# A vision tower on one core: four buffers for a head's exponentials, column copies in pairs, tile list and last side steps moved

## The reference, cut to what matters

```python
for i in range(L):                                   # L = 4 layers, H = 16 heads of 64
    q, k, val = split(h @ W_qkv[i])
    kr = r @ W_r[i]                                  # position keys
    AC = einsum("bqhd,bkhd->bhqk", q + u, k)
    BD = einsum("bqhd,khd->bhqk", q + v, kr)
    prob = softmax((AC + BD) * inv_sqrt_d)           # 257 x 257 for each image and head
    vec = einsum("bhqk,bkhd->bqhd", prob, val)
    h = layer_norm(h + vec @ W_o[i])
    h = layer_norm(relu(h @ W_ff1[i] + b1) @ W_ff2[i] + b2)
...
w = macro_top1 * micro_top2                          # each row: one group of four, its two experts
out = einsum("te,tef,efd->td", w, silu(x @ gate_w[e]) * (x @ up_w[e]), down_w)
```

## Time and profile before

| What | Value |
|---|---|
| Time, median of 3 runs | 2613.9 us (2610.91 to 2614.98) |
| The profiled execution: time, span | 2615.31 us, 2613.5 us |
| PE busy | 2233.3 us, 85% of the span |
| DVE busy | 1846.4 us, 71% |
| ACT busy | 1614.7 us, 62% |
| POOL busy | 1187.9 us, 45% |
| The chain that ended last, by engine | PE 34%, ACT 31%, DVE 11%, issue 7%, POOL 5%, SP's queue 4% |
| Its costliest line | ACT L2144 (exponentials), 12% |
| Mean granted TensorE clock | 0.973 |

### The profile page before, as it was taken

The page is one execution under the profiler, slowest core; times in us unless marked ns, Lnnn a source line. Parts: engine busy times, 40 slices in busy tenths (PEclk is TensorE's granted clock), DMA queues, the critical chain, the costliest instruction groups (busy, mean ns, idle before and its releaser), DMA issues.

```text
span 2613.5 us, 61377 instructions
## 1 busy us (share of the span) xinstructions
PE 2233.3 (85%) x19254; PEld 1641.1 (63%) x19254; DVE 1846.4 (71%) x5687; ACT 1614.7 (62%) x5077; POOL 1187.9 (45%) x2205
## 2 busy tenths in 40 slices
PE   0259999999989999999989999999899999987998
PEld 0136666666766666667656666667666666665565
DVE  8837777777767777777757777777678777776533
ACT  2126667767666677776656667766676766665322
POOL 3025555555456555554544555554565555541211
PEclk9679999999999999999999999999999999998999
DMA  4344444435554343444644444445543343355110
GB/s 162 88 136 112 113 103 105 105 99 145 143 157 119 99 102 102 103 122 132 183 117 115 105 104 104 104 139 143 157 100 91 86 102 90 94 144 178 50 45 22
DMA packets 378062, 295.38 MB, mean 113 GB/s; under 512 B 45087, under 2 KB 350721, under 8 KB 376739
## 3 DMA queue, kind: packets, MB, share of 16 engines
q1 hardware_dynamic: 370603, 272.41, 39.9%
q10 hardware_dynamic: 4864, 12.68, 1.4%
q0 software_dynamic: 2272, 6.35, 0.7%
HBM read 137.71 MB, written 72.07 MB: 80 GB/s over the span
## 4 chain that ended last, share of the span: by engine, by line
PE 34%; ACT 31%; DVE 11%; issue 7%; POOL 5%; SPq 4%; DMA 1%; ACTq 0%; POOLq 0%; DVEq 0%
ACT e_rows L2144 12%; PE bk L2024 6%; PE bk L1898 6%; PE bk L2059 4%; PE bk L1273 4%; ACT pt L2129 4%; SPq L1532 3%; ACT pt L2204 3%; ACT rel L2079 3%; ACT rel L2203 2%; DVE pt L2445 2%; PE bk L2048 2%; POOL arena L1726 2%; PE bk L1886 2%; PE bk L1854 2%
## 5 line engine op out<-in xcount | busy, mean ns | idle before, releaser
L2144 ACT ACTIVATE e_rows<-e_rows,nb 128x257 f32<-128x257 f32 x1024 | 518.0, 519 | 40.8 <-DVE nb L2334 39.9
L2334 DVE CUSTOM_DVE_ANT_0 e_rows<-bk,arena 128x257 f32<-128x257 f32 x1024 | 390.0, 418 | 72.6 <-PE bk L1931 71.4
L1838 PE MATMUL bk<-hin,arena 128*128 128x257 f16 x3072 | 424.0, 275 | 10.2 <-ACT rel L2079 6.6
L2296 DVE TENSOR_TENSOR pt<-bk,pt 128x512 f16<-128x512 f32 x512 | 353.8, 691 | 77.2 <-ACT pt L2129 70.1
L1886 PE MATMUL bk<-ident,e_rows 128*128 128x128 f32 x2048 | 325.0, 281 | 70.7 <-ACT e_rows L2144 52.4
L1724 POOL TENSOR_SCALAR arena<-rel 128x257 f16<-128x257 f32 x496 | 202.6, 409 | 356.2 <-ACT rel L2079 352.0
L1726 POOL TENSOR_TENSOR arena<-rel,arena 128x257 f16<-128x257 f32 x496 | 327.4, 660 | 41.3
L1838 PEld LDWEIGHTS bk<-hin,arena 128*128 128x128 f16 x3072 | 298.1, 98 | 61.2 <-issue 9.2
L1886 PEld LDWEIGHTS bk<-ident,e_rows 128*128 128x128 f32 x2048 | 221.2, 141 | 159.3 <-ACT e_rows L2144 131.4
L2129 ACT ACTIVATE pt<-bk 128x512 f16<-128x512 f32 x512 | 311.6, 609 | 8.1 <-PE bk L1886 8.0
L1774 POOL TENSOR_SCALAR wf<-wf 128x256 f32<-128x256 f32 x216 | 93.0, 431 | 424.6 <-DMA wf<-in_w_dram 254.1
(11 more groups left out here) (328 smaller groups left out, 4278.6 us busy)
## 6 DMA issues: line engine op xcount, KB each, us to landing
arena<-arena SPq DMA_DIRECT2D x768, 128.5 KB
wf<-in_w_dram SPq DMA_DIRECT2D x168, 128.0 KB, 2.9
w_split_dram<-wh SPq DMA_DIRECT2D x168, 128.0 KB, 2.2
xs_dram<-in_c_blank_dram SPq DMA_DIRECT2D x24, 772.5 KB
wf<-in_we_dram SPq DMA_DIRECT2D x96, 128.0 KB, 2.7
we_split_dram<-wh SPq DMA_DIRECT2D x96, 128.0 KB, 1.8
w_rest<-w_split_dram SPq DMA_DIRECT2D x12, 1024.0 KB, 17.0
arena<-we_split_dram SPq DMA_DIRECT2D x8, 1536.0 KB, 11.5
```

Source lines behind the costliest of these rows:

```text
L1838: r_ = mm(bank[4 + s % 2][:, 0:S], wcol(a, C_QKV, k, 3 * HD, chunk_at(s)), hin[:, m, k, :], start=i == 0, stop=i == 5)
L2144: act.activation(E[:, h % 2, qt, :], E[:, h % 2, qt, :], ACT.Exp, bias=nb[:, 2 * h + qt:2 * h + qt + 1], scale=-1.0, accum_out=sums[:, qt, ...
L2296: v.tensor_tensor(pt[:, h, 1, :, 0:IMG], bank[2 + h % 2][:, :].rearrange("p (k s) -> p k s", k=QT), pt[:, h, 0, :, 0:IMG], ALU.subtract).t ...
L2334: v.tensor_tensor_reduce(E[:, h % 2, qt, :], bank[qt][:, 0:S], cb[:, h, :], -SCORE, 3e38, ALU.add, ALU.min, nb[:, 2 * h + qt:2 * h + qt + ...
```

## The change

E gets four buffers (`h % EB`, EB = 4), and DVE waits for the transposes of head h-4 and for the copy of its pair. The column copy is made on odd heads alone, for both heads of a pair in one instruction. To make room, the small tables of the tile list move into the tile that held the position rows (`rT2`), which the last layer doesn't read; the loop that names them is cut below. `first_list` leaves heads 13 to 15 of FINAL and is spread over the value steps c = 0 to 6, two steps each. In the experts' loop several side steps change places.

```diff
+EB = 4
-        E = e_rows[:, 0:2 * QT * S].rearrange("p (b k s) -> p b k s", b=2, k=QT)
+        E = e_rows[:, :].rearrange("p (b k s) -> p b k s", b=EB, k=QT)
...
 # ACT, head h
-                    act.wait_ge(e_ok, at(32, 2 * h + 2))
-                    act.activation(ecol[:, :, class_row(h, 0):class_row(h, 3):4], E[:, h % 2, :, CLS:S].broadcast_to([P, QT, 3]), ACT.Copy).then_inc(ecol_ok, 1)
+                    if h % 2:
+                        act.wait_ge(e_ok, at(32, 2 * h + 2))
+                        both = E[:, (h - 1) % EB:(h - 1) % EB + 2, :, CLS].rearrange("p b k -> p k b").unsqueeze(2).broadcast_to([P, QT, 3, 2])
+                        first, i = class_row(h - h % 4, 0), (h - 1) % 4
+                        act.activation(ecol[:, :, first:first + 12].rearrange("p k (c i) -> p k c i", i=4)[:, :, :, i:i + 2], both, ACT.Copy).then_inc(ecol_ok, 1)
...
 # DVE, head h
-                    if h >= 2:
-                        v.wait_ge(t_done, at(16, h - 1))
-                        v.wait_ge(ecol_ok, at(16, h - 1))
+                    if h >= EB:
+                        v.wait_ge(t_done, at(16, h - EB + 1))
+                        v.wait_ge(ecol_ok, at(8, (h - EB) // 2 + 1))
...
-                    if kind is FINAL and h >= 13:
-                        for k in range(5 * (h - 13), min(5 * (h - 12), experts.LIST)):
-                            experts.first_list(v, k)
...
 # DVE, value step c
                     if c:
                         o_part(at, c - 1)
+                    if kind is FINAL and c < 7:
+                        for k in range(2 * c, min(2 * c + 2, experts.LIST)):
+                            experts.first_list(v, k)
...
 # Experts.vector, tile j
             if j == 3:
                 for k in range(NEWTON):
                     route_newton(v, r, LAST, k)
-                route_normalise(v, r, LAST)
...
             if j + 1 < SLOT_TILES:
                 inner(j + 1, 0)
-            if j == 0:
-                for k in range(WEIGHTS):
-                    route_weights(v, r, LAST - 1, k)
+            if j == 3:
+                route_normalise(v, r, LAST)
             if j == 5:
-                for k in range(WEIGHTS):
+                for k in range(4):
                     route_weights(v, r, LAST, k)
             inner_lo(j, 1)
+            if j + 2 < SLOT_TILES:
+                self.rows_lo(v, j + 2)
             if j == 0:
                 for k in range(SLOTS):
                     route_slots(v, r, LAST - 1, self.side, k)
             if j == 1:
                 add_image()
-            if j + 2 < SLOT_TILES:
-                self.rows_lo(v, j + 2)
             finish(j)
+            if j == 0:
+                for k in range(WEIGHTS):
+                    route_weights(v, r, LAST - 1, k)
...
             if j == 5:
+                for k in range(4, WEIGHTS):
+                    route_weights(v, r, LAST, k)
+            if j == 6:
                 self.next_list(v)
```

More of the change, by code:

```diff
@@ L941, in __init__, with small @@
         self.we = in_arena(keep["arena"], 0, [E_N, E_CHUNKS, 2 * SPLIT])
-        self.steps = sb("steps", [P, CAP + SLOT_TILES + 2 * E_G])
-        self.count = sb("slot_count", [P, E_G])
-        self.cmp = sb("slot_cmp", [P, E_G, SLOT_TILES])
-        self.full = sb("slot_full", [P, E_G])
-        self.used = sb("slot_used", [P, E_G + 1])
-        self.left = sb("slot_left", [P, E_G])
-        self.end = sb("slot_end", [P, E_G])
-        self.spare = sb("slot_spare", [P, E_G])
-        self.tile_f = sb("tile_f", [P, SLOT_TILES])
-        self.tile = sb("tile", [P, SLOT_TILES], I32)
-        self.group_f = sb("group_f", [P, SLOT_TILES])
-        self.group = sb("group", [P, SLOT_TILES], I32)
+        lists = keep["rT2_flat"][:, :].bitcast(F32)
+        place = [0]
+        def small(n):
+            place[0] += n
+            return lists[:, place[0] - n:place[0]]
+        self.steps = small(CAP + SLOT_TILES + 2 * E_G)
+        self.count, self.full, self.left, self.end, self.spare = (small(E_G) for _ in range(5))
+        self.used = small(E_G + 1)
+        self.cmp = small(E_G * SLOT_TILES).rearrange("p (g j) -> p g j", g=E_G)
+        self.tile_f, self.group_f = small(SLOT_TILES), small(SLOT_TILES)
+        self.tile, self.group = (small(SLOT_TILES).bitcast(I32) for _ in range(2))
         self.home = sb("home", [P, 2, 1], I32)
@@ L1403, in attention_stage @@
         vbd = sb("vbd", [P, HD], F16)
-        e_rows = sb("e_rows", [P, 2 * ROW])
-        E = e_rows[:, 0:2 * QT * S].rearrange("p (b k s) -> p b k s", b=2, k=QT)
+        e_rows = sb("e_rows", [P, EB * QT * S])
+        E = e_rows[:, :].rearrange("p (b k s) -> p b k s", b=EB, k=QT)
         ec = sb("ec", [P, S])
@@ L1641, in body @@
                     hold(t_done, at(16, 16))
-                    hold(ecol_ok, at(16, 16))
+                    hold(ecol_ok, at(8, 8))
                     experts.wait_first_list(sp)
@@ L1886, in transposes @@
                         r_ = pe.transpose(bank[2 + h % 2][:, (kt * QT + qt) * P:(kt * QT + qt + 1) * P],
-                                         E[:, h % 2, qt, kt * P:(kt + 1) * P], ident[:, :])
+                                         E[:, h % EB, qt, kt * P:(kt + 1) * P], ident[:, :])
                 r_.then_inc(t_done, 1)
@@ L1986, in body @@
                 pv(at, 1)
-                pe.wait_ge(ecol_ok, at(16, 16))
+                pe.wait_ge(ecol_ok, at(8, 8))
                 pe.wait_ge(rs_ok, at(6, 6))
@@ L2143, in body @@
                         act.wait_ge(s_ok, at(32, 2 * h + qt + 1))
-                        act.activation(E[:, h % 2, qt, :], E[:, h % 2, qt, :], ACT.Exp, bias=nb[:, 2 * h + qt:2 * h + qt + 1],
+                        act.activation(E[:, h % EB, qt, :], E[:, h % EB, qt, :], ACT.Exp, bias=nb[:, 2 * h + qt:2 * h + qt + 1],
                                        scale=-1.0, accum_out=sums[:, qt, h:h + 1]).then_inc(e_ok, 1)
@@ L2333, in body @@
                         v.wait_ge(s_done, s_count)
-                        v.tensor_tensor_reduce(E[:, h % 2, qt, :], bank[qt][:, 0:S], cb[:, h, :], -SCORE, 3e38,
+                        v.tensor_tensor_reduce(E[:, h % EB, qt, :], bank[qt][:, 0:S], cb[:, h, :], -SCORE, 3e38,
                                                ALU.add, ALU.min, nb[:, 2 * h + qt:2 * h + qt + 1]).then_inc(s_ok, 1)
@@ L2526, in vit_tower @@
             held("wm", [P, NP, 32])
-            held("rT2", [P, 2, KC, S], F16)
+            held("rT2_flat", [P, 2 * KC * S], F16)
+            keep["rT2"] = keep["rT2_flat"][:, :].rearrange("p (t k s) -> p t k s", t=2, k=KC)
             held("cc", [P, S])
```

## The result

The changed kernel takes 2587.5 us (median of 4 runs, 2584.05 to 2590.58) where the kernel before takes 2614.44 on the same chip: ratio 0.9906, 95% interval 0.989 to 0.9923, faster by 0.77 to 1.1%. Forecast were 2592.2 us, a gain of 21.7 us, range 2586 to 2600. A second measurement of the same kernel (e10) gave 0.9925 (0.9909 to 0.9941), 2590.77 us beside 2611.01. By the ratios that is 24.6 and 19.6 us; the two together lie around 22 us.

A forecast was written before the change was run, and what follows sets the result against it. ACT was taken to bound MIDDLE's heads, busy 27.97 of 28 us. 14.2 + 1.35 + 1.5 + 3.6 - 0.5 + 1.55 = 21.7 us off 2613.9 gave 2592.2 us, range 2586 to 2600 (chance 0.80).

The forecast's parts named there:

- ACT bounds the heads, a copy costs 0.095 us: MIDDLE, g = 25, OPENING: ACT never waits, so fewer column copies save 0.71 us an iteration, 14.2 us.
- Rival 1 (half): Another engine takes half of all savings: 2603 us; chance 0.09.
- 2 (nothing): The heads don't move at all, only FINAL and the experts gain, 4.65 us: 2609.2 us; chance 0.03.
- 3 (its duration): A column copy costs what its duration shows, 35 instead of 14.2 us saved: 2571 us; chance 0.04.
- 4 (the pattern holds ACT): The pair's four-level copy doesn't overlap; at 0.30 us each the heads lose 17.6 us: 2626.9 us; chance 0.04.
- The room at head 14: DVE's scores at head 14 have 0.10 us of room, of which the removed copy uses 0.09: just enough.
- ENTRY, CLOSING: Heads: ENTRY gains five copies ahead of PE's wait for POOL, three times, 1.35 us; CLOSING, PE-bound, gains nothing.
- four buffers: by themselves nothing: Heads: four buffers alone gain nothing; they only let the pair be copied later.
- TAIL: TAIL's heads: DVE full from about head 5, so only some copies count, 0.3 us five times: 1.5 us.
- The list out of FINAL: FINAL's heads: removing the tile list's steps ahead of PE's waits saves 3.6 us, bounds 2.0 and 4.6.
- The value steps: FINAL's value steps: the list's steps overrun DVE's wait by 0.13 us a step, -0.5 us, bounds nothing and -2.9.
- The experts' side steps: Experts: tile 0 +1.8, tile 5 +1.0, tile 3 -0.95, tile 1 -0.3, together +1.55 us.

The follow-up runs named there:

- e10: The changed kernel itself, measured a second time beside the kernel before: 2590.77 us, ratio 0.9925.
- e3: The kernel before with only the tile list moved from FINAL's heads to its value steps: 2611.56 us, ratio 0.9987.
- e5: The changed kernel with a second copy behind each pair copy, into a tile nobody reads: 2606.29 us, ratio 0.9983 to the kernel before.
- e9: The changed kernel with three experts' side steps placed otherwise and pair copies of heads 1, 11, 13, 15 on POOL: 2583.9 us, ratio 0.9903 to the kernel before.
- e2: The kernel before with four buffers alone, still one copy for every head: 2612.33 us, ratio 0.9993.
- e4: The kernel before with only the experts' side steps in their new places: 2611.85 us, ratio 0.9989.
- e6: The changed kernel with three experts' side steps (tiles 1, 3, 5) placed otherwise: 2588.95 us, ratio 0.9904 to the kernel before.
- e7: The changed kernel with all pair copies on POOL instead of ACT: 2584.74 us, ratio 0.9889 to the kernel before.
- e8: The changed kernel with all pair copies on POOL and e6's edits as well: 2581.52 us, ratio 0.9887 to the kernel before.
- e12: e9's kernel again, unchanged, in other rounds: 2585.17 us, ratio 0.9895 to the kernel before.

## Why the prediction was right, point by point

- **ACT bounds the heads, a copy costs 0.095 us.** Right, and this carried it: 27.82 to 27.13 us is 0.69 for 0.71 forecast, 13.3 us for 14.2 over MIDDLE, g = 25 and OPENING. OPENING gave only 0.15: there ACT waited 1.48 us (0.79 before). One trace can't price it, since it takes 26.88 us in e10's trace of the same kernel, and 28.74 in e3's, where its code is as before. e5 prices a copy at 0.09 to 0.096 us. Rival 1 (half) is out by the 0.69, rivals 2 (nothing), 3 (its duration) and 4 (the pattern holds ACT) are out by e5 and by the two rows of the pair copy.
- **The room at head 14.** "So yes, just" was exact: the changed kernel loses nothing there, and with one copy less (e9) the wait is there.
- **ENTRY, CLOSING.** ENTRY 1.6 for 1.35. CLOSING -0.4 for nothing, nearly all of it at g = 7: 31.30 us, 30.94 and 30.93 at the other two. This isn't scatter. All eleven traces with four buffers, e2's too, have g = 7 longer than g = 23 by 0.35 to 0.4 us, and the three with two buffers (before, e3, e4) have them equal. In g = 7 the exponentials of head 15 come late, since PE's scores do; "four buffers: by themselves nothing" was wrong there by 0.4 us, and why is open.
- **TAIL** was mis-sized: 3.2 us, 1.5 forecast. The step that failed is "DVE is full from about head 5, so the copies of the first heads and that of head 14 count". ACT has no wait before head 14, and each of its pairs up to there is a tenth shorter. That ACT at head 14 still waits 1.24 us says that DVE came earlier by the same amount, so it had been hanging on the others until shortly before. The size is uncertain: in e3 and e4, where nothing of TAIL's heads was changed, it takes 29.46 and 29.42 us and not 29.59, which makes 2.2 to 3.2 us.
- **The list out of FINAL** gave 2.9 in the heads and 1.1 behind, 3.9 for 3.6 forecast (0.2 for copies in it). The size was near but not the reasoning: "so all of it arrives" is false for the list alone (e3: 1.8 us), because DVE stays late without it. "The wait had slowed PE" held: behind the long waits PE's clock stood at 0.50 for 6.8 us. "The transposes at 0.62 again" came true in e10's trace (0.63) and not in the first (1.09), which still had 3.3 us at 0.50. For slow transposes and matmuls 1.0 us had been added; behind the last exponential the first trace gives 1.1 us and e10's 1.6.
- **The value steps** were forecast at -0.5 and cost nothing (7.42 us for 7.41). The steps fill DVE's wait of 0.35 us and take, in four of them, 0.41 to 0.47 us from the first list instruction to the next product, and PE's period of about 1.11 us stays. The loads came no later: from the last value product to PE's first expert matmul 27.24 us, before 27.31.
- **The experts' side steps.** Tile 0 +1.78 (forecast 1.8), tile 5 +1.1 (1.0), tile 3 -0.96 (-0.95), tile 1 -0.29 (-0.3). All four right, the losses too, which e6 takes back. Only the wait at tile 3 is recorded with 0.69 us and not 0.9. From the last value product to the end 1.7 us (1.55).
- **The sum.** 21.7 forecast, 23.3 by the stages of the trace; 26.9 and 20 by the medians of two measurements. 2587.5 us lies near the lower end of the range, 2590.8 inside it. The first holds more than the stages explain: e10 and e2 show that stretches with unchanged code differ by 3 to 8 us from one execution to another, and they do so with PE's clock. The forecast's "scatter of some 2 us between runs" was too small: the 62 executions of the kernel before lie within 16 us, with medians 2.9 us apart between chips. That the sum came so near is luck in part: TAIL's and FINAL's surplus stands against OPENING and CLOSING.

## What to carry to other kernels

On an engine that never waits, price a short instruction from its start to the next start. Then ask for each stage by itself how far the saving reaches: to the next engine's pace, and to the one place where another engine's room is a tenth of a microsecond. Moving work to an engine that is idle on average (POOL, 46% busy) gives back less than counted if it has no gap in just that stretch; a MIDDLE stage lost 0.3 us with all eight copies there (e7) and 0.2 with four (e9); for all eight 0.8 had been counted. In sum the 32 heads stages are hardly shorter for all (900.6 and 904.0 us in e7 and e8) than for half (901.0 and 902.3 in e9 and e12), beside 904.6 in the changed kernel. The clock has a share in that: it fell in five of six ENTRY stages with all copies on POOL and in three of six with half. Edits worth 1 to 3 us can't be seen in times that scatter by more; the intervals between a repeated instruction in the trace show them to 0.05 us. Before two traces are compared by a longer stretch, look at the granted clock of both in it.

## What the runs showed of the hardware

- Durations recorded on ACT overlap: a copy of 6 and one of 12 elements are both recorded with 225 ns, and start 0.09 to 0.11 us before the next. A wait of 0.14 us behind an instruction of 0.65 us appears in no idle bracket; only the distance between starts shows it.
- PE's granted clock stands at either 1.00 (2.4 GHz) or 0.50 (1.2 GHz), and falls for 3 us and more at places that differ between executions of one kernel. Four transposes take 0.63 us at the one and 1.09 at the other; a stretch behind the heads with 3.3 us at 0.50 takes 1.0 to 1.9 us longer than the same one without, over the 14 traces, those between two layers left out. With the same waits ahead of it in FINAL (0.92 and 0.89 us) it fell in the first trace of the changed kernel and not in e10's.
- A copy of 12 elements takes 0.196 us on POOL, the next start 0.15 us behind it, and 0.225 on ACT with 0.10: moved, it costs POOL half as much again as it saves ACT.
